# GpSimd issues a block's six gathers ahead of the second normalisation

## The reference

```python
# edges are sorted by their node (col)
xn   = layernorm(x)
out1 = segment_sum(edge_attr, col)
out2 = where(cnt > 0, segment_max(edge_attr, col), 0)
out3 = out1 / maximum(cnt, 1)
h    = concatenate([xn, out1, out2, out3, u[0]])
x1   = x + xn + relu(h @ W1 + b1) @ W2 + b2
x2   = layernorm(x1)
...
y    = x2 + sum over the 2 best experts of weight * (relu(x2 @ w1[e] + b1[e]) @ w2[e] + b2[e])
out  = x1 + layernorm(y) * gamma + beta
```

## Time and profile before

| | us |
|---|---|
| median of 3 runs | 1422.58 |
| lowest and highest | 1421.58 and 1425.25 |
| the profiled execution | 1423.21 |
| its span, first to last instruction | 1421.5 |
| TensorE matmul busy | 1201.3 |
| VectorE busy | 848.0 |
| GpSimd busy | 795.2 |
| ScalarE busy | 645.1 |
| mean granted clock of TensorE | 0.884 |

### The profile page before, as it was taken

The page is one execution under the profiler, slowest core; times in us unless marked ns, Lnnn a source line. Parts: engine busy times, 40 slices in busy tenths (PEclk is TensorE's granted clock), DMA queues, the critical chain, the costliest instruction groups (busy, mean ns, idle before and its releaser), DMA issues.

```text
span 1421.5 us, 28692 instructions
## 1 busy us (share of the span) xinstructions
PE 1201.3 (85%) x6677; PEld 1015.0 (71%) x6678; DVE 848.0 (60%) x3007; ACT 645.1 (45%) x1969; POOL 795.2 (56%) x1060
## 2 busy tenths in 40 slices
PE   2004998998998999999998254999999999999798
PEld 1003887887887788788887144999999999998343
DVE  5999999999999899000000695344444344443796
ACT  5853555656656556566563000332323232323453
POOL 4874565665665566666751001676766777765122
PEclk7556999999999999999999577999999999999555
DMA  9976677676676656611110823122221222222883
GB/s 314 300 227 246 232 268 268 265 276 262 258 281 260 230 186 236 196 45 42 58 34 30 278 85 133 62 69 74 69 71 63 75 69 71 69 72 58 297 284 102
DMA packets 87468, 231.48 MB, mean 163 GB/s; under 512 B 22145, under 2 KB 34819, under 8 KB 87285
## 3 DMA queue, kind: packets, MB, share of 16 engines
q1 hardware_dynamic: 50401, 167.53, 32.5%
q0 software_dynamic: 26048, 43.47, 10.5%
q10 hardware_dynamic: 10964, 19.96, 4.0%
HBM read 116.42 MB, written 114.25 MB: 162 GB/s over the span
## 4 chain that ended last, share of the span: by engine, by line
PE 54%; DVE 33%; DMA 4%; issue 4%; POOL 2%; ACT 1%; DVEq 1%; SPq 0%; POOLq 0%; ACTq 0%
PE ps L1061 14%; PE ps L1069 14%; DVE mem L1142 12%; DVE mem L1146 12%; PE ps L983 5%; PE ps L969 5%; PE ps L971 5%; PE ps L1089 3%; PE ps L1091 3%; PE ps L1048 2%; DVE mem L1162 2%; DVE mem L1283 1%; DMA mem<-piece_carry,mem 1%; DMA mem<-in_edge_attr_dram 1%; DVE mem L1167 1%
## 5 line engine op out<-in xcount | busy, mean ns | idle before, releaser
L879 ACT ACTIVATE mem<-ps,mem 128x128 f32<-128x128 f32 x452 | 128.8, 368 | 374.8 <-PE ps L1061 374.8
L969 PE MATMUL ps<-mem 128*128 128x250 f32 x800 | 214.1, 391 | 27.2 <-ACT mem L769 25.7
L1061 PEld LDWEIGHTS ps<-mem 128*128 128x128 f32 x1808 | 221.8, 194 | 5.7
L1061 PE MATMUL ps<-mem 128*128 128x128 f32 x1808 | 222.2, 277 | 0.0
L1069 PE MATMUL ps<-mem 128*128 x904 | 213.8, 379 | 0.4 <-issue 0.4
L1142 DVE TENSOR_TENSOR_SCAN mem<-ps,mem 128x80 f32<-128x80 f32 x960 | 207.9, 303 | 0.3
L971 PE MATMUL ps<-mem 128*128 128x250 f32 x800 | 208.1, 383 | 0.0
L1146 DVE TENSOR_TENSOR_SCAN mem<-ps,mem 128x80 f32<-128x80 f32 x960 | 207.8, 308 | 0.0
L621 POOL DMA_INDIRECT expert_rows<-mem x113 | 138.2, 1223 | 113.3 <-DVE mem L1317 66.0
L969 PEld LDWEIGHTS ps<-mem 128*128 128x128 f32 x800 | 156.2, 198 | 47.5 <-ACT mem L769 27.4
L983 PE MATMUL ps<-mem 128*125 128x256 f32 x800 | 180.9, 379 | 0.7 <-ACT mem L769 0.7
(11 more groups left out here) (206 smaller groups left out, 1785.6 us busy)
## 6 DMA issues: line engine op xcount, KB each, us to landing
run_sum<-mem SPq DMA_DIRECT2D x40, 960.0 KB
run_max<-mem SPq DMA_DIRECT2D x40, 960.0 KB, 7.6
mem<-in_edge_attr_dram SPq DMA_DIRECT2D x36, 960.0 KB, 10.3
mem<-in_L_ffn_w_dram SPq DMA_DIRECT2D x32, 512.0 KB, 9.7
mem<-expert_rows SPq DMA_DIRECT2D x22, 512.0 KB, 6.0
x_rows<-mem ACTq DMA_DIRECT2D x25, 256.0 KB, 2.0
x_normed<-mem ACTq DMA_DIRECT2D x25, 256.0 KB, 2.8
mem<-in_x_dram ACTq DMA_DIRECT2D x24, 256.0 KB, 7.8
```

The source lines that it names most:

```text
L879: ins = act.activation(hT[b][:, c, :], bank(2 + b, c * P, (c + 1) * P), ACT.Relu, bias=eb1c[:, bass.ds(e, 1), c])
L969: pe.matmul(h, W1x[:, c, hc * P:(hc + 1) * P], XT[b][:, c, :], start=(c == 0), stop=False)
L1061: ins = pe.matmul(bank(2 + b, f * P, (f + 1) * P), w1now[b][:, c, f * P:(f + 1) * P], XgT[b][:, c, :], start=(c == 0), stop=(c == DC - 1))
```

## The change

In `rows_step` the call of `gather(i+2)` moves from behind `norm2(i-1)` to ahead of it. Nothing else is changed: same instructions, same semaphores, same buffers. Both calls are there in steps 1 to 22.

```diff
@@ -577,10 +577,10 @@
                     cut(*after(i, g, b))
                     norm1(i + 1)
                     join(*after(i, g, b))
+                if not isinstance(i, int) or i + 2 < MACROS:
+                    gather(*after(i, g, b, 2))
                 if norm:
                     norm2(i - 1)
-                if not isinstance(i, int) or i + 2 < MACROS:
-                    gather(*after(i, g, b, 2))
             pool.sem_inc(joined, 1)
             gather(0, 0, 0)
             norm1(0)
```

## The result

The changed kernel takes 1524.05 us (median of 4 runs, 1514.65 to 1524.55) against 1423.35 us (4 runs). The ratio is 1.069, with a 95% interval of 1.065 to 1.074: 6.9% slower. Its profiled execution took 1524.55 us with a span of 1522.8. The forecast was 1556 with a range of 1500 to 1580.

The account below looks back on a forecast made before the run. TensorE bounds the kernel; the change makes a loop through GpSimd, ScalarE and TensorE set 21 periods of 32.1 us instead of 24.42: L995 of step 22 +130.9, last clock price 2.5, 1423.2 + 133.4 = 1556.6, said as 1556; range 1500 to 1580.

Parts of the forecast that it names:

- parts 1 and 2: Steps 1 to 22, join's end to L995: 15.31 us against 10.3 of room; the 5.0 us TensorE stall repeats.
- gather section: On GpSimd: value load, copy, branches and six issues, 12.14 us, put between join and norm2.
- handover: From the end of norm2 through ScalarE's write_x2 to TensorE's L995: 1.24 us, read at the tail.
- The loop: GpSimd, ScalarE, TensorE: L995 to add_rows 5.07, to join's end 9.25, to L995 15.31; 29.63 us without clock price.
- part 3: TensorE at L995 and layer2's second half: each stall also drops the clock, 2.5 us more, making the period 32.1.
- rival (b): Low clock covers all of L995 and layer2's second half, +4 us a period, or gathers land late: 1589; chance 0.08.
- part 4: At cut: late-gather waits, 33.6 us, vanish but don't come off the sum; norm2 behind gather's own waits costs 0.
- Rival (a): TensorE's clock stays up through most stalls in the block loop, or its price hides: +79.0, 1502 us; chance 0.09.
- Rival (c): Between join and L995: early issue cures late landings and norm2 still fits, gather section under 7.1 us: 1390; chance 0.04.
- prize of 33.6 us: Block loop, 21 periods: what the stage lost to late gather landings above 512.8 us in the kernel before.

Follow-up runs that it names:

- experiment 1: The changed kernel with 18 or 9 filler matmuls a step on TensorE where it stands still ahead of L995: 1574.69 us with 18, 1496.60 us with 9.
- fill9: The changed kernel with 9 filler matmuls a step on TensorE where it stands still ahead of L995: 1496.60 us, ratio 1.053 to the kernel before.
- norm2_after_3: Against the kernel before, norm2 is called behind three of the six gather issues, with three following it: 1422.93 us, ratio 1.002.
- head_ahead: Against the kernel before, only gather's value load, wait for the turned block and index copy stand ahead of norm2: 1400.15 us, ratio 0.985.

## Why the prediction was right, and where it was off

**The path from `join` to L995 (parts 1 and 2): right.** The mechanism, its place and its repetition in 22 steps are what the trace shows. Of the 15.31 us, the steps behind 625.83 give 11.41 to L554 (12.34 forecast), 1.77 for `norm2` (1.73), and 1.63 to L995 (1.24): 14.81. The gather section was read 0.9 us too long. In the kernel before, the first issue comes 3.2 us behind the end of `norm2` (644.41 to 647.62); behind `join` it comes after 2.4. The handover was read 0.4 us too short, because the tail from which I took it (1.24) is written out without a loop: in steps 1 and 22 of the changed kernel, written out too, it takes 1.29 and 1.36, in the looped steps between them 1.57 to 1.63. The two errors partly cancel, which is luck.

**The loop.** From L995 at 640.64 to `add_rows` at 647.33 are 6.69 us (5.07 + 2.5 forecast), to the end of `join` at 656.40 another 9.07 (9.25). The average of the 21 periods is 30.74 us instead of 32.1, and this makes up most of the miss: 21 x 1.36 = 28.6 us. 2.5 more come from step 1 (L995 at 179.06, forecast 181.6) and 0.8 from the period behind step 22, which is 26.1 instead of 26.9. Together 31.9 of the 32 us.

**The clock (part 3): mechanism right, size too large.** I took 2.5 us a period from waits ahead of `layer1`; experiment 1 gives 1.63. That is 18 of the 28.6 us. With 1.63 I would have said 1538. The granted clock of the stage is 0.94, not near 0.9, and the low clock covers L995 and the first six of 16 records, not the whole second half as rival (b) had it. What speaks for a price of this size is `fill9`. What the Trainium skill says in "TensorE: Matmul & The Clock Gate", section "What's actually happening", that the ramp penalty is under 1% of a typical span, isn't borne out here: 27 us between the changed kernel and `fill9` are 1.8% of 1524, and this is with nine more matmuls a step. That sentence stands in a passage on the slow matmuls at a kernel's start; here the price came in each of 22 steps. The measured 1524 lies nearer to the 1516 that the prediction worked out from it than to my 1556, so the time alone would not have settled this; `fill9` does.

**What is given back (part 4): right.** No reordered step has a wait for gathers: the time from the last issue to `cut` is 13.2 to 14.1 us (14.6 forecast). A quarter of the edge loads changed nothing in the changed kernel. `norm2` behind the gather's own waits cost nothing: no L520 has SyncE's queue as its releaser in the changed kernel's trace.

**Rival (a)**, the clock stays up, gave 1502: `fill9`, in which it does, took 1496.6. The forecast's range reached down to 1500 and so took in rival (a)'s time too; the measured time by itself doesn't part them well, that run does. **Rival (c)**, faster, is half confirmed: it put the deciding point at a gather section of 7.1 us ahead of `norm2`, and the run with three gathers, where `norm2` starts 7.1 us behind `join`, is the last that costs next to nothing. But that run gained nothing either (1422.93). The prize of 33.6 us came only with the head ahead and a `cut` that waits for four gathers.

## What to carry to other kernels

An in-order engine with time to spare on average can still hold a short result that another engine waits for: measure the room from the end of the common predecessor to the start of the waiting instruction, and set against it all that is put in between, issues and branches too. Then follow the delay around the loop; if it comes back to its start, it is paid every time, and a stall that drops TensorE's clock is paid for twice (here 4.4 us and 1.63 us). To get the gathers earlier here, the time in which the engine waits anyway was the place (the head of the next one's work), and a consumer that waits for less at once.

## What the runs showed of the hardware

- A matmul of `layer2` has two records in the trace. 18 fillers left 36 records and took 7.9 us; counting records as instructions had me size the fillers at half their length. The "four matmuls" of L969 in the prediction are four records of two matmuls too; the durations read from them stand.
- In the kernel before, the six late gathers of the 21 periods landed 6.1 to 9.6 us behind the end of their last issue; over all runs the latest took 11.7 (`norm2_after_3`). With 13.2 us or more between the last issue and `cut` in the changed kernel none was late.
- The price in clock of a short wait of TensorE varies, and the runs don't show why: in `head_ahead` five waits of 1.5 to 1.9 us cost between 0.1 and 1.9 us beyond themselves; the regular 4.4 us of the changed kernel cost 1.63 on average.
